# Half of the raw attention scores of eight node tiles move from the attention stage into the front stage, by way of DRAM

## What is computed

```python
q = (h @ Wq).reshape(n, H, DK)            # h = layernorm(x), n = 1250, H = 8 heads, DK = 64
k = (h @ Wk).reshape(n, H, DK)
v = (h @ Wv).reshape(n, H, DK)
e = jnp.einsum('ehd,ehd->eh', k[src], q[dst]) / np.sqrt(DK)
ex = jnp.exp(e - segment_max(e, dst)[dst])
attn = ex / segment_sum(ex, dst)[dst]
a = segment_sum(attn[:, :, None] * v[src], dst).reshape(n, 512)
```

## Time and profile before

| what | us |
|---|---|
| median of 3 runs | 1842.4 |
| lowest and highest run | 1840.17, 1845.6 |
| the profiled execution | 1840.33 |
| its span, first to last instruction | 1838.7 |
| front, to the first instruction of the count | 234.2 |
| count of edges | 234.2 to 313.5 |
| attention | 313.9 to 619.6 |

### The profile page before, as it was taken

The page is one execution under the profiler, slowest core; times in us unless marked ns, Lnnn a source line. Parts: engine busy times, 40 slices in busy tenths (PEclk is TensorE's granted clock), DMA queues, the critical chain, the costliest instruction groups (busy, mean ns, idle before and its releaser), DMA issues. The chain is left out here.

```text
span 1838.7 us, 31262 instructions
## 1 busy us (share of the span) xinstructions
PE 1587.7 (86%) x9860; PEld 1166.1 (63%) x9860; DVE 959.0 (52%) x1950; ACT 702.3 (38%) x1610; POOL 559.2 (30%) x638
## 2 busy tenths in 40 slices
PE   3991067999999998899999999659999999898994
PEld 2540045888888656558999999645555555655662
DVE  8520088767676576460000000259999999542233
ACT  2220055655556333443112221255555555432331
POOL 6777701010110121260000000135555554133133
PEclk7996588999999998799999999869999999998997
DMA  6200011710120300658555660176555554629985
GB/s 183 62 7 6 7 44 47 250 24 12 22 85 1 90 1 1 242 157 320 205 200 217 231 228 32 55 202 175 156 157 155 155 156 140 219 52 306 343 264 182
DMA packets 127656, 247.75 MB, mean 135 GB/s; under 512 B 34356, under 2 KB 51608, under 8 KB 123084
## 3 DMA queue, kind: packets, MB, share of 16 engines
q1 hardware_dynamic: 88204, 166.69, 27.1%
q0 software_dynamic: 39360, 79.86, 15.2%
HBM read 196.03 MB, written 50.40 MB: 134 GB/s over the span
## 5 line engine op out<-in xcount | busy, mean ns | idle before, releaser
L2067 PE MATMUL acc<-prod,ohy 128*64 128x256 f32 x1056 | 248.7, 386 | 7.1 <-DVE prod L2185 7.1
L2111 ACT ACTIVATE ohy<-oh,RECS 128x64 f32<-128x64 f32 x704 | 187.0, 336 | 151.0 <-PE acc L2067 151.0
L2067 PEld LDWEIGHTS acc<-prod,ohy 128*64 128x64 f32 x1056 | 138.4, 138 | 131.7 <-issue 70.1
L2044 POOL DMA_INDIRECT rows<-up_dram,idx x176 | 166.9, 948 | 143.9 <-DVE prod L2185 101.5
L1821 DVE TENSOR_SCALAR FT<-y_ps,b2T 128x188 f32<-128x188 f32 x32 | 13.2, 414 | 320.7 <-PE y_ps L1770 320.7
L271 POOL DMA_INDIRECT rec_dram<-recs,pos x157 | 161.2, 1027 | 59.8 <-issue 48.3
L2070 PE MATMUL acc<-prod,ohy 128*64 128x256 f32 x704 | 177.3, 395 | 0.0
L2185 DVE TENSOR_TENSOR prod<-w_ps,rows 128x768 f32<-128x768 f32 x176 | 167.3, 950 | 0.0
L1758 PE MATMUL hid_ps<-FT,W 128*128 128x188 f32 x1024 | 165.5, 323 | 0.8 <-ACT FT L1795 0.8
L1770 PE MATMUL y_ps<-hid,W 128*128 128x188 f32 x1024 | 164.5, 323 | 0.0
L1758 PEld LDWEIGHTS hid_ps<-FT,W 128*128 128x128 f32 x1024 | 163.1, 190 | 0.9 <-issue 0.9
(11 more groups left out here) (389 smaller groups left out, 2653.0 us busy)
## 6 DMA issues: line engine op xcount, KB each, us to landing
W<-in_L_ffn_w SPq DMA_DIRECT2D x16, 4096.0 KB, 16.2
bankW_sp<-in_L_ffn_W_sp SPq DMA_DIRECT2D x2, 4096.0 KB, 23.2
h_dram<-h3e SPq DMA_DIRECT2D x22, 256.0 KB, 4.4
h<-h_dram SPq DMA_DIRECT2D x22, 256.0 KB, 2.9
QF<-q_dram SPq DMA_DIRECT2D x20, 250.0 KB
xin_sp<-zeros SPq DMA_DIRECT2D x1, 4352.0 KB, 21.3
xin_fq<-zeros SPq DMA_DIRECT2D x1, 4352.0 KB, 31.0
b2B<-in_L_ffn_b_sp SPq DMA_DIRECT2D x17, 256.0 KB, 7.0
```

What stands on the lines that cost most here:

```text
L2044: pool.indirect_dma_start(out=rows[:, t, :], out_offset=None, in_=up_dram, in_offset=bass.IndirectOffsetOnAxis(ap=idx[:, par, t:t + 1], ax ...
L2067: upper = lambda m: nc.tensor.matmul(acc[0:HALFB, bank, :].rearrange("p (b c) -> p b c", c=MUL)[:, m:4:3 - m, :], ohs[:, 1 + m, :], pr[:, ...
L2111: last = nc.scalar.activation(ohy[:, t % OHY, i, :], oh[:, par, t, :], ACT.Copy, scale=RECS[:, bass.ds(BATCH * g + t, 1), 4 + i])
```

## The change

In the front, when the projections are done, TensorE also forms the raw scores (no mask yet) of heads 1, 3, 5 and 7 of tiles 0 to 7, 32 in all. The queries come back from `q_dram` into the space of `QT`, and are split by ScalarE (upper part) and VectorE (lower part). Raw scores are copied from PSUM by ScalarE (even ones) and VectorE (odd ones) into four slots that lie in `X`; `X` itself has been stored in `x_dram`. SP stores 28 of the 32 to `raw_dram`; the last four, tile 0's, stay in `X`. The waits at the front's end grow by these stores, and after the front the semaphores used so far are cleared, with a barrier.

In attention the odd heads of tiles 0 to 7 have no scores. Their mask, exponential and turn run in place in the four slots, which SP refills from `raw_dram`. The other heads use `S` in turn. After head 64 SP brings `X` back, and only then loads the parameters. The loops on TensorE and ScalarE are written out. The zero fill moves from attention's SP queue to that of the count. The diff, cut:

```diff
@@ front
+                with ExitStack() as projecting:
+                    W = [tile_in(projecting)(f"Wqkv{i}", [128, KC, DIM]) for i in range(3)]
+                QS = [sb(f"QS{u}", [128, 2, RAW_HEADS, P], F32R) for u in range(4)]
...
 sync
+                        sp.wait_ge(applied, TILES)
+                        for p0, p1 in TILE_PARTS:
+                            sp.dma_start(x_dram[p0:p1], X[p0:p1]).then_inc(x_stored, 16)
...
+                        for k in range(RAW_TILES):
+                            i = (k + 1) % RAW_TILES
+                            if k >= 4:
+                                sp.wait_ge(q_split, k - 3)
+                            for half in range(2):
+                                sp.dma_start(QF[k % 4][DK * half:DK * (half + 1)], q_dram[:, 1:HEADS:2, P * i:P * (i + 1)]
+                                             ).then_inc(q_back[k % 4], 16)
+                        for n in range(RAWS - 4):
+                            sp.wait_ge(raw_moved[n % 2], n // 2 + 1)
+                            for p0, p1 in TILE_PARTS:
+                                sp.dma_start(raw_dram[n, p0:p1, :], in_x[n % 4][p0:p1]).then_inc(raw_stored[n % 4], 16)
...
 vector
+                        def split_lower(k):
+                            dve.wait_ge(upper_split, k + 1)
+                            nc.vector.tensor_tensor(QS[k % 4][:, 1], QF[k % 4], QS[k % 4][:, 0].bitcast(F32), ALU.subtract
+                                                    ).then_inc(q_split, 1)
...
+                        for n in range(1, RAWS, 2):
+                            dve.wait_ge(raw_scored, n + 1)
+                            if n >= 4:
+                                dve.wait_ge(raw_stored[n % 4], 32 * (n // 4))
+                            nc.vector.tensor_copy(in_x[n % 4], raw_ps[1][:, 0:NODES]).then_inc(raw_moved[1], 1)
...
 tensor
+                        for n in range(RAWS):
+                            k, h = n // RAW_HEADS, n % RAW_HEADS
+                            pe.wait_ge(q_split, k + 1)
+                            if n >= 2:
+                                pe.wait_ge(raw_moved[n % 2], n // 2)
+                            for c0, cn in CHUNKS:
+                                for part in range(2):
+                                    last = nc.tensor.matmul(raw_ps[n % 2][:, c0:c0 + cn], QS[k % 4][:, part, h, :],
+                                                            KT[:, 2 * h + 1, c0:c0 + cn], start=part == 0, stop=part == 1)
+                            last.then_inc(raw_scored, 1)
@@ count_edges, sync
                         stage(sp, 0)
+                        fill_rows(sp)
@@ attend, sync
-                        zeros_in = fill_zeros(sp, xin0[0:EXPERTS * ROWS0, :], zeroed)
-                        for bank in BANKS:
-                            zeros_in += fill_zeros(sp, xin1[bank], zeroed)
...
+                                for j in range(RAW_HEADS * i, RAW_HEADS * (i + 1)):
+                                    sp.wait_ge(turned, 2 * (2 * (j - 4) + 2))
+                                    for p0, p1 in TILE_PARTS:
+                                        sp.dma_start(in_x[j % 4][p0:p1], raw_dram[j - 4, p0:p1, :]).then_inc(raw_in[j % 4], 16)
+                        sp.wait_ge(turned, 2 * MIXED)
+                        for p0, p1 in TILE_PARTS:
+                            sp.dma_start(X[p0:p1], x_dram[p0:p1]).then_inc(x_back, 16)
                         sp.wait_ge(masked, HEADS * EARLY)
                         load_params(sp)
@@ attend, tensor
-                            if after >= 2:
-                                pe.wait_ge(masked, n + 2)
...
+                            if after >= 2 and n + 2 in scored_at:
+                                pe.wait_ge(masked, older[n + 2] + 1)
+                                scores(n + 2)
@@ attend, vector
+                                out=place_of[n], in0=score_ps[:P, 0:NODES] if n in scored_at else place_of[n],
+                                in1=masks(2 * pairs - 2 + par),
@@ the calls
             front(KT, V, turnI, spotI, endI)
+            recycle()
```

More of the change, by code:

```diff
@@ L129, in gnn_moe_gnn_moe @@
         zeros = sb("zeros", [128, DIM])
+        SLOT = TILES * DIM // 4
+        in_x = [X[:].rearrange("p t d -> p (t d)")[:, SLOT * u:SLOT * u + NODES] for u in range(4)]
         count = sb("count", [128, 128])
@@ L597, in dense_params, with count_edges @@
             return sems, (Wo, W1, W2, g1, s1, g2, s2, b2, braw, Wraw, biasB), load
-        def count_edges(masks, stage, split, turnI, spotI, endI):
+        def count_edges(masks, stage, split, turnI, spotI, endI, fill_rows):
             HALFN = NODES // 2
@@ L731, in _, with attend @@
                                                      ACT.Copy).then_inc(evicted, 1)
-        def attend(KT, V, masks, T, QS, tiles_scored, q_split, stage, split, load_params):
+        def attend(KT, V, masks, T, QS, tiles_scored, q_split, stage, split, load_params, rows_filled):
             with ExitStack() as st:
@@ L740, in attend @@
                 spread, lifted, deepened = sems_in(st)("inverse_spread", "values_lifted", "mask_deepened")
-                (zeroed,) = sems_in(st)("rows_zeroed")
+                (x_back,) = sems_in(st)("x_back")
+                raw_in = sems_in(st)(*[f"raw_in{u}" for u in range(4)])
                 S = sb("S", [P, 2, NODES])
@@ L846, in step @@
                                 pe.wait_ge(probs_ready, n + 2)
-                                turn((h + 1) % HEADS)
+                                turn(n + 1)
+                        scores(0)
                         pe.sem_inc(normed, 1)
-                        scores(0, 0, 1)
-                        pe.wait_ge(masked, 1)
-                        scores(0, 1, 1)
                         pe.wait_ge(probs_ready, 1)
                         turn(0)
[L856 to L859, removed]
+                        for r in range(TILES // 2):
+                            two_tiles(r, step, r == 0, r == TILES // 2 - 1)
                         pe.wait_ge(copied, 2 * HEADS * TILES)
@@ L2791, in gnn_moe_gnn_moe, with fill_rows, rows_filled @@
             QS, tiles_scored, q_split, stage, split = query_tiles(attention)
-            count_edges(masks, stage, split, turnI, spotI, endI)
-            attend(KT, V, masks, FT, QS, tiles_scored, q_split, stage, split, load_params)
+            (zeroed,) = sems_in(attention)("rows_zeroed")
+            zero_rows = [xin0[0:EXPERTS * ROWS0, :], *[xin1[bank] for bank in BANKS]]
+            def fill_rows(sp):
+                for target in zero_rows:
+                    fill_zeros(sp, target, zeroed)
+            def rows_filled(sp):
+                sp.wait_ge(zeroed, sum(16 * (2 if target.shape[0] % 128 else 1) for target in zero_rows))
+            count_edges(masks, stage, split, turnI, spotI, endI, fill_rows)
+            attend(KT, V, masks, FT, QS, tiles_scored, q_split, stage, split, load_params, rows_filled)
         with ExitStack() as moe:
```

84 lines of the change are left out of this document (65 added, 19 removed).

## The result

The changed kernel takes 1828.9 us (median of 5 runs, 1826.8 to 1831.5) against 1840.2 in the same session: ratio 0.9935, 95% interval 0.9916 to 0.9954, a gain of 8 to 15 us. The forecast was 1816, range 1804 to 1830: the time lies in the range, but the gain, 11 us by the medians, is less than half of the 25.5 that the sum had. The profiled execution took 1830.46 us with a span of 1828.8.

The account below looks back on a forecast made before the run. GpSimd's scatters bound the front, VectorE the count and TensorE attention. Terms -28 + 1.5 + 1 = -25.5 us took the profiled 1840.33 to 1814.8, or 1817 from the runs' median; forecast 1816 us, range 1804 to 1830.

Parts of the forecast that it names:

- Zero fill in the count: The fill, moved from attention's first 30 us to run beside the count's VectorE work, is covered there: cost 0.
- rival (c): The count slows under the zero fill, its engines fetching indices from SBUF: 10 us, about 1825; chance 0.03.
- Attention, the gain: In tiles 0 to 7 a pair of heads lasts 6.52 us instead of 7.46: 28 us over 30 pairs.
- The front: Raw scores and stores before attention end by about 231 us, at no cost; scatter delays and clearing cost 1.5 and 1.
- delayed scatters: In the front, eight new VectorE subtractions may each delay one GpSimd scatter: 0 to 3 us, taken as 1.5.
- clearing and barrier: Semaphore clearing and barrier after the front cost between 0 and 1.5 us, taken as 1.
- ring estimate of 47 us: In the front, raw stores through four slots take 7 rounds of 6.7 us, 47 us, ending near 203.
- bounds of 244 and 395: DMA rates in GB/s for the front's 28 raw stores: 72 us, ending near 230, or 44 us.
- (a): Raw stores bind the front's end, their rows spread unevenly over engines: +9 us, about 1822; chance 0.13.
- (b): VectorE's raw copies in the front slow the scatters too: 13 us, about 1829; chance 0.06.
- (d) to (f): No odd-step wait, about 1799, chance 0.04; attention's gain eaten, 1838 to 1842, 0.06; slow store landings, about 1862, 0.10.
- The sum: Whole kernel: -28 for attention, +1.5 for scatters, +1 for clearing, -25.5 us in all.

Follow-up runs that it names:

- e2: The kernel before with only the zero fill moved from attention into the count: 1848.5 us, ratio 1.0037 to the kernel before.
- e1: The changed kernel with the zero fill moved from the count to late attention, behind the parameter loads: 1822.9 us, ratio 0.9884 to the kernel before.
- e7: The changed kernel with the zero fill moved from the count into the front: 1823.3 us, ratio 0.9886 to the kernel before.
- e8: e7 plus idle-time matmuls at attention's start, written into a free PSUM bank: 1817.7 us, ratio 0.9868 to the kernel before.
- e9: e8 with nine tiles' odd heads instead of eight computed in the front, 32 raw stores instead of 28: 1812.6 us, ratio 0.984 to the kernel before.
- e3: The changed kernel's front with attention and zero fill as before, raw scores stored but never read: 1844.8 us, ratio 1.001 to the kernel before.
- e5: The changed kernel with the fill's zeros read from DRAM instead of SBUF, still in the count: 1824.1 us, ratio 0.9899 to the kernel before.
- e6: The changed kernel with PE loading indices once for two sets, eight values per load: 1829.0 us, ratio 0.9918 to the kernel before.

## Why the prediction was wrong

**The step that failed** is "Zero fill in the count": cost 0, with the words "Its cover is the whole count". It is rival (c), to which I gave 0.03 because "nothing in the rows speaks for it". I had named its mechanism, indices fetched from SBUF. It costs 6.8 us by e2's runs and 6.4 by its count, where the rival had 10; without it (e1, e7) the ratio is 0.005 lower, about 9 us, with intervals of some 5 us either way. The mistake was to take a transfer as covered because DMA and time were free, when an engine with no slack to lose reads its indices from the memory that the transfer reads. VectorE was busy for 75.04 of 79.8 us, so any delay of PE beyond its idle time shows.

**Attention, the gain**, was right as a mechanism: tile 26.18 for 26.1, the turn 5.38 us behind the scores (391.62 to 397.00) for 5.41, PE's wait before it released by ScalarE's copy, no odd mask waiting for its load. That wait is 0.24 us in the mean, not 0.55, since PE itself reaches the turn later than I had it; the chain sets the length of the pair all the same. Once a tile an odd mask, now with two inputs in SBUF, takes 2.05 us instead of 1.45, always beside GpSimd's query split; that costs at most 0.1 us a tile (such a pair lasts 6.62 us, the next 6.52). The size, 28, came out at 24.2 (305.9 - 281.7). I had counted the pairs from step 3 and left out what happens ahead of them: with head 1's scores gone, PE idles in the first steps and runs them at half clock, 24.3 us to the scores of head 6, where 21 would follow from 21.96 before (partly at the lower clock as well) less 0.94. e8, with that time filled, gains 29.7, in part by a better start. How slow the start is varies by execution: 20.3 to 24.3 us without the idle-time matmuls.

**The front** was costed at 1.5 for delayed scatters and 1 for clearing and barrier; the profile has 3.5 and 0.7. The 1.5 was right in kind: in the nine kernels with the subtractions 25 scatters are lengthened, to 1.01 to 1.46 us, and each of them starts while a subtraction runs and ends some 0.84 us after it. Scatters that were already running, or beside the raw copies, keep their 0.97. The sum is 0.3 us in the changed kernel, where two are hit, and up to 1.5 (e9, five). DVE's row for the second of the two:

```profile
190.25 0.67 DVE L417 TENSOR_TENSOR QS<-QT,QS 128x500 fp32r<-128x500 f32 x1
```

The remark in the Trainium skill, "SBUF — State Buffer", section "Who interferes with whom", that tensor_tensor was not seen to stall descriptor writing, would make it 0; these traces do not bear it out. What the prediction lacked is the 114th scatter, which waits 3.6 us longer than before. What exactly it waits for no run tells: of the two waits that the program has among the scatters, one stands ahead of every 16th, which the 114th is not, and the other is for projections, which ended at 146 us; no code load lies between 160 and 180 us in the trace.

**The stores.** My ring estimate of 47 us was too short. The 28 stores are issued from 153.51 to 215.6, 2.2 us each, 0.625 MB / 2.2 = 284 GB/s between my bounds of 244 and 395, and both copying engines wait for them. The waits of DVE and ACT from 150 to 225 us:

```profile
DVE X L426 <- DMA raw_dram<-X: 43.9, 14, 6.3
...
ACT X L524 <- DMA raw_dram<-X: 41.6, 12, 4.9
```

That they end by 231, and so cost nothing directly, was right; e9 shows the room that was left. Rivals (a), (b) and (d) to (f) did not come. **The sum** as measured: -24.2 + 4.2 + 6.4 = -13.6, which lies in the interval of the result (-8 to -15). That takes the fill from e2 and the front from the profile (e3's runs have 0 to 3.7 for it); with the 3.3 of the changed kernel's own count it is -16.7, a little outside. Of the 11.9 us between this and the forecast, 6.4 are the fill, 3.8 attention, most of it the start (24.3 - 21), and 1.7 the front.

## What to carry to other kernels

A transfer that finds free DMA time is not free yet: look at which engine loads registers from SBUF meanwhile, and put a bulk fill beside work that loads no indices (e1, e7), or source it from DRAM (e5). When work is taken from a busy engine, look at the first steps, where it may now stand idle and run at the lower clock, and fill its idle time where that holds nothing up. This move into a gap could be taken further than the first version did (e9); the room is the time from the last transfer to the end of what bounds the gap.

## What the runs showed of the hardware

Ahead of a set PE stands still for some 0.21 to 0.24 us for each index value that it loads from SBUF while a 395 GB/s transfer reads SBUF (e6 and the changed kernel). How long the load itself takes no row shows. Without the transfer there is no such wait beside PE's 0.24 us for VectorE. The matmuls and VectorE's instructions keep their length beside it (1.27 us a set, 0.42 and 1.26 us): here the traces agree with the Trainium skill, "SBUF — State Buffer", section "Who interferes with whom", that DMA never contends with a compute engine, but PE as a whole did lose time.

The fill from DRAM to DRAM kept the DMA engines as busy at 314 GB/s, and cost the count nothing.

A scatter that GpSimd starts while VectorE subtracts two SBUF tiles ends some 0.84 us after the subtraction instead of 0.97 after its own start (25 in nine kernels, all that began over 0.15 us before the subtraction's end but one, which began together with it); a scatter that was already running is not lengthened.

One scatter of 157, always the 114th, waits 1.68 us where the scatters alone use the DMA queues and 3.4 to 5.8 in the kernels with raw stores.
